# Decay mixer: four chunks of the depthwise convolution as multiply-adds on VectorE, none as diagonal products on TensorE

## What is computed

```
xz = layernorm(x) @ W_in                      # 256 -> 1024
xc, z = split(xz)                             # 512 channels each
xc[t] = sum_{w=0..3} conv_w[:, w] * xc[t + w - 3]   # per channel, causal
xc = layernorm(silu(xc), gamma, beta)
xp = xc @ W_xproj                             # 512 -> 33: one delta, 16 B, 16 C
decay = clip(exp(delta * A), 1e-6, 1)         # 16 x 512 values per position
y = xc * sum_n(B*C*decay) + xc * D
x = x + (y * silu(z)) @ W_out
```

## Time and profile before

| | |
|---|---|
| median of 3 runs | 3248.37 us (3245.37 to 3250.24) |
| the profiled execution | 3246.3 us, span 3244.5 us |
| mean granted TensorE clock | 0.933 |
| busy shares of the span | TensorE 86%, VectorE 65%, ScalarE 50%, GpSimd 32% |

### The profile page before, as it was taken

How to read it: one execution, slowest core, us unless ns; L and a number is a source line. 1 busy time by engine, 2 the same in 40 slices (tenths; PEclk the granted TensorE clock), 3 DMA queues, 4 the chain that set the end, 5 groups by cost and what they waited for, 6 DMA issues and landing times.

```text
span 3244.5 us, 40490 instructions
## 1 busy us (share of the span) xinstructions
PE 2797.3 (86%) x13782; PEld 1683.0 (52%) x13782; DVE 2111.5 (65%) x3830; ACT 1625.4 (50%) x2437; POOL 1024.4 (32%) x714
## 2 busy tenths in 40 slices
PE   7777887887755799999969999968889988999999
PEld 4444444554443455555635666534444445666666
DVE  1788888888885677777522222246766675777776
ACT  3778777777861355555431111148777681111111
POOL 0788888888781221121010000011121000010000
PEclk9899999999877899999979999979988898999999
DMA  3587887788873775555331000010000002000000
GB/s 111 119 175 146 172 175 164 146 178 168 160 173 79 192 186 90 91 82 91 53 141 59 23 23 25 28 38 7 7 12 9 1 1 59 7 14 7 7 7 13
DMA packets 119272, 262.94 MB, mean 81 GB/s; under 512 B 14784, under 2 KB 72896, under 8 KB 117408
## 3 DMA queue, kind: packets, MB, share of 16 engines
q0 software_dynamic: 24928, 134.89, 20.0%
q1 hardware_dynamic: 94144, 125.47, 16.9%
HBM read 135.40 MB, written 131.20 MB: 82 GB/s over the span
## 4 chain that ended last, share of the span: by engine, by line
PE 50%; ACT 7%; issue 6%; DVE 4%; DMA 1%; SPq 0%; POOL 0%; POOLq 0%; ACTq 0%; DVEq 0%
PE PS L2404 7%; PE PS L1677 6%; PE PS L2422 6%; PE PS L1975 4%; ACT Z L2133 3%; PE PS L1699 3%; PE PS L1340 2%; PE PS L2025 2%; PE PS L1297 2%; PE PS L1319 2%; PE PS L1983 2%; PE PS L1322 2%; PE PS L1267 2%; PE PS L2007 1%; PE PS L1366 1%
## 5 line engine op out<-in xcount | busy, mean ns | idle before, releaser
L856 POOL TENSOR_TENSOR Z<-Z 128x1024 f32<-128x1024 f32 x256 | 647.9, 2758 | 131.0 <-DVE Z L757 78.3
L764 DVE TENSOR_TENSOR_SCAN Z<-PS,Z 128x1024 f32<-128x1024 f32 x256 | 576.3, 2274 | 21.8 <-ACT PS L684 11.7
L535 PE MATMUL PS<-Z 128*128 128x128 f32 x2048 | 304.9, 295 | 124.7 <-DVE Z L764 50.3
L535 PEld LDWEIGHTS PS<-Z 128*128 128x128 f32 x2048 | 250.5, 151 | 256.3 <-issue 81.2
L684 ACT ACTIVATE PS<-Z 128x511 f32<-128x511 f32 x512 | 332.7, 687 | 65.5 <-DVE Z L764 63.7
L1436 ACT ACTIVATE Z<-PS 128x512 f32<-128x512 f32 x320 | 188.9, 596 | 262.7 <-PE PS L1322 257.3
L2455 ACT ACTIVATE Z<-PS 128x512 f32<-128x512 f32 x144 | 85.9, 596 | 415.5 <-PE PS L2404 415.5
L696 ACT ACTIVATE Z<-PS,Z 128x512 f32<-128x512 f32 x378 | 245.5, 683 | 78.5 <-PE PS L535 70.9
L2404 PE MATMUL PS<-Z 128*128 128x512 f32 x576 | 275.3, 604 | 7.9 <-DVE Z L2537 7.1
L1529 DVE TENSOR_REDUCE Z<-PS 128x1 f32<-128x512 f32 (+2 forms) x384 | 182.7, 507 | 116.4 <-PE PS L1298 111.6
L487 PE MATMUL PS<-Z 128*128 128x512 f32 x512 | 244.2, 606 | 10.3 <-ACT Z L604 9.5
(11 more groups left out here) (297 smaller groups left out, 4959.9 us busy)
## 6 DMA issues: line engine op xcount, KB each, us to landing
sums<-Z POOLq DMA_DIRECT2D x112, 768.0 KB, 7.8
Z<-rows_b SPq DMA_DIRECT2D x128, 256.0 KB, 4.4
Z<-scr SPq DMA_DIRECT2D x256, 128.0 KB, 5.3
rows_n<-in_L_ffn_expert_wv POOLq DMA_DIRECT2D x32, 528.0 KB, 7.7
scr<-Z SPq DMA_DIRECT2D x32, 384.0 KB
Z<-Z POOLq DMA_DIRECT2D x14, 768.0 KB, 7.5
Z<-in_L_ffn_expert_wv SPq DMA_DIRECT2D x4, 2048.0 KB, 15.5
Z<-sums SPq DMA_DIRECT2D x7, 768.0 KB, 6.6
```

The lines of the kernel that those rows point to most:

```text
L535: ins = e.transpose(self.turned[i % 2][:, c * 128:(c + 1) * 128], self.h(k, c // 2)[:, c % 2, i * 128:(i + 1) * 128], ident)
L764: e.tensor_tensor_scan(h, a, h, 0.0, ALU.mult, ALU.add).then_inc(s["scan"], 1)
L856: e.tensor_tensor(self.h(k, f), self.du[b % 2][:, 2 * f:2 * f + 2, :], b3(self.Bs[k % 2], 1, [128, 2, 512]), ALU.mult).then_inc(s["hin"], 1)
```

## The change

Chunks 0 and 1 of the convolution move from `conv`/`conved` to `taps`. The diagonal matrices and the code that makes them go, and so do two uses of the PSUM ring in each batch. The two tables of the order, and the places in `END`, are dealt out anew: the lifts now stand in the order 0 to 7, at most one to a slot.

```
-        self.diag = ar.take([2, 4, 128])
...
     PLAN = (
         (("stats",),), (("rstd",), ("minus",)), (("norm",),), (("flip", 0), ("flip", 1)),
-        (("flipped", 0), ("flipped", 1), ("lift", 2)), (("lifted", 2), ("lift", 3)), (("taps", 2), ("lift", 0)),
-        (("lifted", 3), ("lifted", 0), ("taps", 3), ("lift", 1)), (("lifted", 1), ("conv", 0)),
-        (("conved", 0), ("conv", 1)), (("lift", 4), ("conved", 1)), (), (("lifted", 4),),
-        (("lift", 5), ("lifted", 5), ("lift", 6), ("lift", 7)), (("lifted", 6), ("lifted", 7), ("silu",)),
+        (("flipped", 0), ("flipped", 1), ("lift", 0)), (("lifted", 0), ("lift", 1)), (("taps", 0), ("lifted", 1)),
+        (("lift", 2),), (("lifted", 2), ("taps", 1), ("lift", 3)), (("lifted", 3), ("lift", 4)),
+        (("taps", 2), ("lifted", 4), ("lift", 5)), (("lifted", 5), ("lift", 6)),
+        (("taps", 3), ("lifted", 6), ("lift", 7)), (("lifted", 7),), (("silu",),),
         (("turnx", 0), ("turnx", 1), ("turnx", 2), ("turnx", 3)), (("stats2",),), (("rstd2",), ("xn", 3)),
...
     START = (
-        (("stats",), ("consts",)), (("rstd",), ("minus",), ("spread",)), (("norm",), ("decay",)), (("flip", 0), ("flip", 1)),
-        (("flipped", 0), ("flipped", 1), ("lift", 2)), (("lifted", 2), ("lift", 3)),
-        (("lifted", 3), ("taps", 2), ("lift", 0)), (("lifted", 0), ("taps", 3), ("lift", 1)), (("bound",),),
-        (("lifted", 1), ("conv", 0)), (("conved", 0), ("conv", 1))) + (
-        (("conved", 1), ("lift", 4)), (("lifted", 4), ("lift", 5)), (("lifted", 5), ("lift", 6)),
-        (("lifted", 6), ("lift", 7)), (("lifted", 7), ("silu",)),
+        (("stats",), ("consts",)), (("rstd",), ("minus",)), (("norm",), ("decay",)), (("flip", 0), ("flip", 1)),
+        (("flipped", 0), ("flipped", 1), ("lift", 0)), (("lifted", 0), ("lift", 1)),
+        (("lifted", 1), ("taps", 0), ("lift", 2)), (("lifted", 2), ("taps", 1), ("lift", 3)),
+        (("lifted", 3), ("lift", 4)), (("taps", 2), ("lifted", 4), ("lift", 5)), (("taps", 3), ("lifted", 5), ("lift", 6)),
+        (("lifted", 6), ("lift", 7)), (("lifted", 7),), (("silu",), ("bound",)),
...
-    END = ((3, "wout"), (5, "turnw"), (7, "gate"), (9, "proj"), (11, "acc"))
+    END = ((4, "wout"), (5, "turnw"), (7, "gate"), (8, "proj"), (9, "acc"))
...
-        def conv(b, c):
-            e.wait_ge(s["consts"], 1)
-            e.wait_ge(*ring.done(self.use("lift", b, c)))
-            o = bank("conv", b, c)
-            for w in range(4):
-                ins = e.matmul(o, self.diag[:, c, w, :], self.xp[:, c, w:w + 512], start=w == 0, stop=w == 3)
-            ins.then_inc(s["prod"], 1)
...
         def silu(b):
-            for c in range(2):
-                e.wait_ge(*ring.done(self.use("conv", b, c)))
-            e.wait_ge(s["conv"], 2 * b + 2)
+            e.wait_ge(s["conv"], 4 * b + 4)
...
         def consts(b):
             e.wait_ge(s["pads"], 1)
-            for c in range(2):
-                for w in range(4):
-                    e.tensor_scalar(self.diag[:, c, w, :], m.ident, vec["conv1"][:, 4 * c + w:4 * c + w + 1], None, ALU.mult)
-
-        def spread(b):
             for j in range(4):
```

More of the change, by code:

```diff
@@ L1874, in __init__ @@
         for step in self.steps:
-            if step[0] in ("flip", "lift", "conv", "turnx", "back", "xproj", "rep"):
+            if step[0] in ("flip", "lift", "turnx", "back", "xproj", "rep"):
                 self.uses[step] = len(self.uses)
@@ L2044, in proj @@
             ins.then_inc(s["op"], 1)
-        self.walk(flip=flip, lift=lift, conv=conv, turnx=turnx, back=back, xproj=xproj, rep=rep, sum=sums, turnw=turnw,
+        self.walk(flip=flip, lift=lift, turnx=turnx, back=back, xproj=xproj, rep=rep, sum=sums, turnw=turnw,
                   proj=proj)
@@ L2139, in wout @@
             e.activation(self.wt[w % 2], self.wb[w % 2], ACT.Copy).then_inc(s["wt"], 1)
-        self.walk(decay=decay, rstd=rstd, norm=norm, flipped=flipped, lifted=lifted, conved=conved, silu=silu, rstd2=rstd2, xf=xf,
+        self.walk(decay=decay, rstd=rstd, norm=norm, flipped=flipped, lifted=lifted, silu=silu, rstd2=rstd2, xf=xf,
                   soft=soft, grow=grow, wout=wout)
@@ L2256, in acc @@
             e.tensor_tensor(m.X[:, w, :], m.X[:, w, :], self.ob[:, 0:256], ALU.add).then_inc(s["acc"], 1)
-        self.walk(consts=consts, spread=spread, bound=bound, add=add, stats=stats, minus=minus, taps=taps, stats2=stats2, xn=xn, pj=pj, clip=clip, scalars=scalars,
+        self.walk(consts=consts, bound=bound, add=add, stats=stats, minus=minus, taps=taps, stats2=stats2, xn=xn, pj=pj, clip=clip, scalars=scalars,
                   scale=scale, gate=gate, acc=acc)
```

## The result

The changed kernel takes 3199.91 us, median of four runs (3196.64 to 3210.43), against 3249.3 us of the kernel before (four runs, 3245.37 to 3251.26). The medians are 49.4 us apart. The ratio of the runs is 0.9855, 95% interval 0.983 to 0.988, so the changed kernel is 1.45% faster. The profiled execution took 3200.01 us, its span is 3198.2.

What follows compares the result with a forecast made beforehand. No engine is full; TensorE's and ScalarE's stretches in series bound each batch. Six periods -32.4, start -6.0, clock +1.5 make -36.9 us, so 3211 us; forecast 3200 to 3221 (0.55), 8-in-10 range 3197 to 3232.

Steps and rivals of the forecast that it cites:

- (1): Settled batch: two conv leave TensorE's stretch, -7.26 us, so that stretch is 38.2 us.
- (2): Settled batch: one grow and one wout ahead of silu lengthen ScalarE's stretch by 1.8 us to 24.4.
- (3), (5): Two conved copies leave ScalarE off the path; proj and acc come one and two slots earlier: both at nothing.
- (4): Two more taps add 5.6 us a batch to VectorE, 52.9 busy; hidden with 1.6 us slack, so nothing.
- (6): Start, batch 0 without its convs: first grow 5.4 us earlier, one copy less 0.6; -6.0 us.
- (7): Last 19 grows after the last xproj hang on ScalarE: nothing; stage five moves as a whole.
- (8): TensorE's clock: more pauses, three slow periods of six in place of two, +1.5 us.
- B: Rival: the clock eats a part; all six periods slow 3222, with slow lifts 3242; chance 0.13.
- C: Rival: VectorE becomes the bound; its instructions 10% longer give 3233; chance 0.10.
- E: Rival: ends slower by the clock alone, half clock lasting to the end of the lifts, 3329; chance 0.05.
- F: Rival: no change, an unseen wait takes the place of the convs, 3248; chance 0.05.
- D: Rival: more gained, added grow and wout hidden or clock stays up; 3199, without slow periods 3193; chance 0.12.

Runs made afterwards that it cites:

- two pairs of traces: Kernel before and changed kernel, each traced a second time without edits: 3253.98 us and 3202.42 us in the repeat.
- The early silu: Changed kernel with silu and the transposes behind it one slot earlier in each batch but the first: 3198.7 us, ratio 0.9854.
- the two doses: Changed kernel with eight, then twenty, unread VectorE multiplies added a batch behind taps 3: 3203.0 us and 3249.6 us.

## Why the prediction was right, point by point

The time lies in the range, the sign and the mechanism are as forecast, and the gain was a third larger than the 36.9 us worked out, so that the time stands at the lower edge of the forecast's own 3200 to 3221. The mixer gave 44 to 45.5 us of it in the two pairs of traces. The other 5 to 6.5 us lie in stage five, whose clock was higher; the forecast had no term for that, and that it went the right way is luck as far as these runs show. By its own steps:

(1) *TensorE's stretch, 38.2 us.* It is 37.2. The 7.3 us count in full. The further 1.0 is clock: flips, the sum behind them (0.99 in place of 1.86) and `xproj` ran at full clock and took 1.5 us less than in the batch that the prediction copied, and the rest of the stretch took 0.5 more than that batch's.

(2) *ScalarE's stretch, 24.4 us.* It is 24.5, with the grow waiting for the sum and the `wout` ahead of silu. The early silu shows that this is no mistake of the new order that could be undone: the work has to be done somewhere in the stretch.

(3), (5) *Nothing for the copies and the finishing steps.* No wait on them appears on the path; the `wout` is counted in (2).

(4) *VectorE covered, slack 1.6 us.* Covered, and the instructions last what the trace of before said (52.2 us busy for 52.9). The slack was some 1.8 us by the two doses. The walk had VectorE 0.2 us late at `stats2`; the trace has it waiting there 1.07 us, because `rep` ended 16.2 us after the flips in place of 17.5. The multiply-adds don't overlap, as the prediction can be read: three of 752 ns take 2.33 us. What the walk did show rightly is that the order keeps this cover: in the old order it is gone.

(6) *The start, -6.0.* It was -3.4 to the flips of batch 2 in the first pair of traces and -0.5 in the second; from the first flips to the first grow -2.7 and +1.2. So the term gave 3.4 us or less of its 6.0, and the periods made up for it. The prediction had charged the add and statistics ahead of `xn`, but not that TensorE would then pause 9.3 us and run `xproj` in 5.7 us in place of 3.7. Two empty slots bring the first grow 7 us nearer to the first flips.

(7) *The tail, nothing.* -0.4. *Stage five moves as a whole*: it moved and took 6.5 us less (4.7 in the second pair), with the same code and a higher clock.

(8) *The clock, +1.5.* This is the term that was mis-sized, and with the wrong sign. The prediction took three slow periods in place of two, and there was none: `xproj` took 3.69 us in the chain above, against 6.97 in the earlier trace rows. Six periods of 24.4 + 38.2 make 375.6 us, 35.9 under the 411.5; the trace has 371.0, 40.5 under. The prediction had 32.4 less 1.5. The forecast of more pauses was wrong too: TensorE idles 7.3 us in the period shown (61.6 less 54.3) and idled 7.0 before, not 2.2 us more. The mean clock of the whole mixer is 0.88 in both kernels: it was not higher, but the low stretches lay off the path. In the settled batch of before one of them lay over the flips and the sum (0.5 to 4.0 us after the first flip) and one over lift 0 (7.4 to 10.8); now only lift 0 is hit (5.9 to 9.3). The prediction's sign, a mean clock under 0.93, held of both kernels and so told nothing. The Trainium skill, TensorE: Matmul & The Clock Gate, Part 1, has it that activity releases the throttle. By that rule as the prediction used it, longer pauses meant more matmuls at half clock. The trace agrees for the fall behind the pause of 4.5 us, which went when the pause was filled; but that one lay off the path, and the fall behind `xproj` came with the pause filled too.

Of the rivals, B, C, E and F did not come about; D named the size (3199) but half of it for a reason that is false: the grow and the `wout` are not hidden. The rest was the clock on the path.

What stays open: why the falls of the clock met less of the path in both traces of the changed kernel, what besides narrow matmuls the fall behind `xproj` takes, and why stage five has two durations. The 4.4 us ahead of the mixer are of one execution; the medians carry them or not by chance.

## What to carry to other kernels

Cut the stage into the stretches of its chain and ask in which one the removed work lies: 7.3 us off TensorE's stretch were worth 7.3, while reordering inside ScalarE's stretch was worth nothing. When work moves to a less busy engine, its total tells only whether it can fit; whether it does hangs on its place in that engine's queue, and the same multiply-adds gave 27 us in the old order and 49 in the new one. Before you read a slack off a period that did not get longer, look whether something else in it got shorter: eight added instructions seemed free, and a faster lift had paid for them. Take durations for the sum from rows at a known clock, and let the clock's own term reach to both sides of nothing. A mean clock says little; ask which work on the path the low stretches hit.

## What the runs showed of the hardware that was not expected

The clock fell while TensorE was busy without a gap, behind 3.7 us of 128x33 matmuls, and the 128x512 lift after them took 3.5 us for 1.8. With three 128x256 matmuls in between it stayed at 1.00 there, and the lift took 1.96 us, in all seven batches. The same 3.7 us were not followed by a fall in six of seven batches of the kernel with eight added VectorE instructions, so they alone don't decide it. The fall after a pause of 4.5 us could be removed by filling the pause, and the other one came all the same.
